# ScalarE copies the turned row maxima, first-pass slots are repacked and spread over the step, two value products stand together

## The reference

```python
scores = jnp.einsum('bqhd,bkd->bhqk', q, k) * scale
slopes = _alibi_slopes(nH)
alibi = slopes[:, None, None] * (pos_k - pos_q).astype(jnp.float32)
scores = jnp.where(causal[None, None], scores + alibi[None], NEG_INF)
probs = jax.nn.softmax(scores, axis=-1)
attn = jnp.einsum('bhqk,bkd->bqhd', probs, v).reshape(B, S, H)
return attn @ Wo
...
x = x + _L0_attn_ref(_layernorm(x, axis=-1), L0_attn_Wqkv, L0_attn_Wo)
x = x + _L0_ffn_ref(_layernorm(x, axis=-1), L0_ffn_W_base, L0_ffn_b_base, L0_ffn_W_gate, L0_ffn_A, L0_ffn_B)
```

## Time and profile before

| What | Before |
|---|---|
| Median of 3 runs | 703.57 us (703.44 to 704.35) |
| Profiled execution | 700.96 us |
| Its span in the trace | 699.2 us |
| TensorE busy | 669.7 us (96%) |
| VectorE busy | 557.4 us (80%) |
| ScalarE busy | 358.6 us (51%) |
| GpSimd busy | 216.9 us (31%) |
| Granted TensorE clock | 1.0 of full speed |

### The profile page before, as it was taken

One profiled execution on the slowest core, in us unless ns is written; L12 is line 12 of the kernel. 1 busy time (PEld: TensorE's weight loads), 2 busy tenths in 40 slices (PEclk: granted clock), 3 DMA queues, 4 the chain that ended last, 5 costly groups with the idle time before them and its releaser, 6 DMA issues.

```text
span 699.2 us, 13261 instructions
## 1 busy us (share of the span) xinstructions
PE 669.7 (96%) x4304; PEld 305.5 (44%) x4304; DVE 557.4 (80%) x1801; ACT 358.6 (51%) x511; POOL 216.9 (31%) x366
## 2 busy tenths in 40 slices
PE   3889999999999999999999999999999999999997
PEld 2434344544344444444443343433433455555553
DVE  5899889887989889898988989899881365666565
ACT  2324647567556676666666666767667411111111
POOL 0035424233332515243352231422432412222220
PEclk9999999999999999999999999999999999999999
DMA  8578108080411443080144744225200189700001
GB/s 253 130 145 137 64 2 136 30 147 28 166 54 51 60 89 108 11 131 34 41 63 94 102 81 77 49 49 94 48 18 33 52 130 170 162 30 30 31 30 60
DMA packets 42951, 56.32 MB, mean 81 GB/s; under 512 B 6648, under 2 KB 26232, under 8 KB 42752
## 3 DMA queue, kind: packets, MB, share of 16 engines
q1 hardware_dynamic: 40296, 51.27, 37.3%
q10 hardware_dynamic: 2592, 4.26, 1.8%
HBM read 35.72 MB, written 19.79 MB: 79 GB/s over the span
## 4 chain that ended last, share of the span: by engine, by line
PE 83%; DVE 10%; DMA 3%; ACT 2%; issue 1%; SPq 1%; POOL 0%; DVEq 0%; ACTq 0%; POOLq 0%
PE psum L780 20%; PE psum L732 18%; PE psum L762 13%; PE psum L808 8%; PE psum L830 7%; PE psum L678 7%; PE psum L759 5%; DVE psum L1145 3%; PE psum L825 2%; PE psum L840 2%; ACT work L965 2%; DMA x_sb<-in_x 1%; DVE negm L1150 1%; PE psum L817 1%; DMA arena<-q_dram 1%
## 5 line engine op out<-in xcount | busy, mean ns | idle before, releaser
L965 ACT ACTIVATE work<-psum 128x1024 f32<-128x1024 f32 (+1 forms) x320 | 289.0, 943 | 127.6 <-PE psum L762 108.5
L1145 DVE CUSTOM_DVE_ANT_0 psum<-psum,future 128x384 f32<-128x384 f32 (+3 forms) x512 | 237.7, 514 | 12.6 <-PE psum L732 10.4
L732 PE MATMUL psum<-k_op,arena 106*128 106x512 bf16 (+3 forms) x768 | 212.4, 328 | 9.6 <-DVE negm L1145 4.3
L1150 DVE TENSOR_REDUCE negm<-psum 128x1 f32<-128x512 f32 x256 | 168.6, 687 | 15.3 <-PE psum L732 10.9
L1318 POOL TENSOR_SCALAR_AFFINE_SELECT work<-work 128x512 f32<-128x512 f32 x128 | 81.2, 634 | 296.2 <-ACT work L965 296.2
L780 PE MATMUL psum<-work,v_op 128*32 128x512 f32 (+3 forms) x1536 | 163.5, 498 | 0.5 <-POOL work L1318 0.4
L762 PE MATMUL psum<-arena,k_op 109*128 109x512 bf16 (+3 forms) x640 | 157.3, 316 | 1.9 <-ACT work L965 0.8
L732 PEld LDWEIGHTS psum<-k_op,arena 106*128 106x128 bf16 x768 | 69.0, 97 | 128.5 <-DVE negm L1145 40.7
L678 PE MATMUL psum<-arena,wqkv_sb 128*128 128x256 f32 (+3 forms) x240 | 84.6, 453 | 1.1 <-ACT arena L887 1.1
L759 PE MATMUL psum<-arena,k_op 116*128 116x128 bf16 x512 | 84.3, 221 | 0.9 <-ACT work L965 0.9
L762 PEld LDWEIGHTS psum<-arena,k_op 109*128 109x128 bf16 x640 | 59.6, 98 | 44.5 <-ACT work L965 15.7
(11 more groups left out here) (86 smaller groups left out, 454.8 us busy)
## 6 DMA issues: line engine op xcount, KB each, us to landing
arena<-q_dram SPq DMA_DIRECT2D x96, 128.0 KB, 5.5
o_dram<-o_sb SPq DMA_DIRECT2D x32, 256.0 KB
q_dram<-arena SPq DMA_DIRECT2D x16, 384.0 KB, 4.4
arena<-o_dram SPq DMA_DIRECT2D x32, 128.0 KB, 4.6
arena<-rcp_dram SPq DMA_DIRECT2D x32, 128.0 KB, 4.9
out<-wqkv_sb ACTq DMA_DIRECT2D x16, 256.0 KB, 2.0
x_sb<-in_x SPq DMA_DIRECT2D x3, 1024.0 KB, 10.0
work<-in_x SPq DMA_DIRECT2D x3, 1024.0 KB, 18.8
```

The source lines that it names most:

```text
L732: last = nc.tensor.matmul(bank[:, a * width:(a + 1) * width], q_op[0:ROW_MAX, bass.ds(col, P)], k_op[0:ROW_MAX, b, k0:k0 + width], start=T ...
L965: nc.scalar.activation(probs[:, n % 4, heads * hp:heads * (hp + 1), 0:w], src, ACT.Exp).then_inc(exp_done, 1)
L1145: last = nc.vector.tensor_tensor_reduce(keys, keys, future[:, CH - width:CH], -1.0, 3e38, ALU.add, ALU.min, negm[:, late, 0, j * QT + t:j ...
L1150: nc.vector.tensor_reduce(dst, psum[:, bank, 0:len(js) * width].rearrange("p (a k) -> p a k", a=len(js)), AX_X, ALU.max, negate=True).then ...
```

## The change

- ScalarE copies the turned maxima (line 956) in place of VectorE, with semaphores of their own (`turn_full`, `turn_done`). The turns (line 758) are no longer slots: the early one stands behind slot 12, the late one of step k behind the third slot of step k+1, and that of the last unit ahead of step 16. A turn holds one of the three slot banks until ScalarE has copied.
- The minimum of line 1128 goes: the diagonal reduces of the late unit (line 1176) take the full block's maximum as their starting value, one column of `negm`, in place of the constant 3e38, and wait for the slot that wrote it.
- A step has 36 slots in place of 42. Diagonal blocks (j, 2) and (j, 0) share a bank, as do (j, 1) and (j+1, 1); (j, 3) stands alone. The matmuls and the columns reduced are the same.
- `SLOTS_BY` goes from 0.95 to 1.02.
- In the frame of `pe_order` the value products of the tiles with 256 and with 128 queries per head stand as one block.

The lines move: 732 becomes 746, 713 becomes 758, 759 and 762 become 782 and 785, 780 becomes 803, 965 becomes 1005, 1145 and 1150 become 1176 and 1183.

```diff
-SLOTS_BY = 0.95
+SLOTS_BY = 1.02
...
+    full = [[("full", late, ((j, t),)) for j in range(UH)] for t in range(QT)]
+    pairs = [("diag", late, ((j, 1), (j + 1, 1))) for j in range(0, UH, 2)]
+    uneven = [("diag", late, ((j, 2), (j, 0))) for j in range(UH)]
+    wide = [("diag", late, ((j, 3),)) for j in range(UH)]
+    if not late:
+        return uneven + pairs + wide
+    return full[0] + full[1] + pairs + full[2] + uneven + full[3] + wide
...
-TURN = [EARLY_SLOTS + TURN_AFTER, len(SLOTS) + 1]
-SLOTS.insert(TURN[0], ("turn", 0, None, None))
-SLOTS.insert(TURN[1], ("turn", 1, None, None))
...
+def turn_behind(k, put):
+
+
+    if put == EARLY_SLOTS + TURN_AFTER[0]:
+        return [("turn", 2 * k, None)]
+    if put == TURN_AFTER[1] and k:
+        return [("turn", 2 * k - 1, None)]
+    return []
...
-            work.append((UH * (CH - TILES[v][2]) + PV_FIXED, ("values", m, v)))
+            for tile in {2 * P: (), P: (v - 1, v)}.get(CH - TILES[v][2], (v,)):
+                work.append((UH * (CH - TILES[tile][2]) + PV_FIXED, ("values", m, tile)))
...
+            def turn_maxima(u):
+
+
+                bank, before = TURN_BANK[u]
+                bank_free(before)
+                pe.wait_ge(slot_free, NSL * (u // 2) + (NSL if u % 2 else EARLY_SLOTS))
+                nc.tensor.transpose(psum[0:UH * QT, bank, 0:P], negm[:, u % 2, 0, :], ident[:]).then_inc(turn_full, 1)
...
+            def copy_maxima(u):
+
+                act.wait_ge(turn_full, u + 1)
+                if u >= 2:
+
+                    act.wait_ge(m_split, u - 1)
+                nc.scalar.copy(m_t[:, u % 2], psum[0:UH * QT, TURN_BANK[u][0], 0:P]).then_inc(turn_done, 1)
...
-                            nc.vector.tensor_tensor(negm[:, 1, 0, :], negm[:, 1, 0, :], negm[:, 1, 1, :], ALU.min
-                                                    ).then_inc(max_late, 1)
...
+                    if k and r in (0, EARLY_SLOTS):
+
+                        dve.wait_ge(turn_full, 2 * k - 1 + late)
...
+                                last = nc.vector.tensor_tensor_reduce(keys, keys, future[:, CH - width:CH], -1.0,
+                                                                  negm[:, 1, 1, to:to + 1] if late else 3e38, ALU.add, ALU.min,
+                                                                  negm[:, late, 0, to:to + 1])
...
-                pool.wait_ge(slot_free, at_loop(NSL * (u // 2) + TURN[u % 2] + 1, i, 2 * NSL))
+                pool.wait_ge(turn_done, u + 1)
```

More of the change, by code:

```diff
@@ L165, in vector_time @@
 def vector_time(k, r):
-    kind, _, t, _ = SLOTS[r]
-    time = 450 if kind == "turn" else 680 if kind == "full" else (550, 750, 500, 700)[t]
+    kind, _, parts = SLOTS[r]
+    time = 680 if kind == "full" else sum((275, 375, 500, 700)[t] for _, t in parts)
     if r in KEY_SLOTS.get(k, ()):
@@ L217, in pe_order @@
         done += w
-        while k < NK and put < NSL - 1 and slot_due(k, put) * total <= done:
+        while k < NK and put < NSL and slot_due(k, put) * total <= done:
             out.append(("slot", k, put))
             put += 1
+            out += turn_behind(k, put)
         out.append(piece)
-    return out + [("slot", k, r) for r in range(put, NSL if k < NK else 0)]
+    for r in range(put, NSL if k < NK else 0):
+        out.append(("slot", k, r))
+        out += turn_behind(k, r + 1)
+    return ([("turn", NU - 1, None)] if k == NK else []) + out
 ORDER = [pe_order(k) for k in range(NK + 2)]
 def places():
-    slot_at, use_at, last = {}, {}, [None] * NSB
+    slot_at, use_at, turn_at, last = {}, {}, {}, [None] * NSB
     for u in range(N_FIRST):
@@ L241, in places @@
                 banks.append(bank)
+            elif what == "turn":
+                bank = banks.pop(0)
+                turn_at[a] = (bank, last[bank])
+                last[bank] = ("turn", a)
+                banks.append(bank)
             elif what == "side" and a >= N_FIRST:
@@ L267, in uses_behind @@
             piece = b
-        if what == "side" and b == len(use_parts(USES[a])) - 1:
-            out.setdefault(piece, []).append(a)
+        if what == "turn" or what == "side" and b == len(use_parts(USES[a])) - 1:
+            out.setdefault(piece, []).append((what, a))
     return out
@@ L653, in bank_free @@
                     pe.wait_ge(slot_free, n + 1)
+                elif what == "turn":
+                    pe.wait_ge(turn_done, n + 1)
                 else:
@@ L792, in step @@
                         max_slot(m, n)
+                    elif what == "turn":
+                        turn_maxima(m)
                     elif what == "scores":
@@ L1117, in _, with step @@
             KEY_PIECES = 7
-            def step(k, i=None, some=range(NSL)):
+            def step(k, some=range(NSL)):
                 for r in some:
-                    kind, late, t, js = SLOTS[r]
+                    kind, late, parts = SLOTS[r]
                     idx = NSL * k + r
                     bank = SLOT_AT[k, r][0]
-                    if kind == "turn":
-                        u = 2 * k + late
+                    if k and r in (0, EARLY_SLOTS):
+                        dve.wait_ge(turn_full, 2 * k - 1 + late)
+                    dve.wait_ge(slot_full, idx + 1)
+                    if kind == "diag":
@@ L1135, in step @@
[L1135 to L1146 removed]
+                            dve.wait_ge(slot_free, NSL * k + max(SLOTS.index(("full", 1, (part,))) for part in parts) + 1)
```

85 lines of the change are left out of this document (34 added, 51 removed).

## The result

The changed kernel takes 706.54 us (median of 6 runs, 705.61 to 708.18), the kernel before 703.41 in the runs beside it (6 runs, 702.69 to 704.35). The ratio is 1.0058, with a 95% interval of 1.0045 to 1.0071: slower by 3.2 to 5.0 us. The profiled execution took 705.61, its span is 703.8.

What follows compares the result with a forecast made beforehand. TensorE's own work was taken to set nearly all the time. Late steps +0.2, projection steps +0.55 and the loose steps with step 16 -0.1 made about +0.7 us: median 703.57 to 704.3, range 700.2 to 708.6.

Steps and rivals of the forecast that it cites:

- the likeliest case: Whole kernel: waits that go and waits that come cancel, 704.3 us, own range 702.2 to 705.8; chance 0.42.
- C: Rival, slower by VectorE: at 0.143 us a late reduce, slots come late, +0.5 a late step, 708.5 us; chance 0.15.
- 1.24 us of waits at four places: TensorE in late steps: 0.49 at (1,0), 0.30 at (5,0), 0.15 at slot 4, 0.30 at slot 30.
- +0.04: Late steps 10 to 15: 1.24 us of new waits, less 0.2 for joining, against 1.0 before; +0.04 each.
- The joined products: Value products on TensorE: one pair per step without a slot between, none in steps 1 and 2, saves 0.2 us each.
- +0.11: Projection steps 5 to 9: 0.91 us of new waits, less 0.2 for joining, against 0.6 before; +0.11 each.
- The column operand: VectorE's 16 late diagonal reduces a step read one more column: 0.06 us each, 1.0 a step.
- B: Rival, faster: the column operand hides in the reduce's own read, VectorE loses 0.85 us a step, 700.6 us; chance 0.28.
- The late maxima: Copy, split, store and load ahead of (4,0): slack shrinks from 2.87 us to 0.7, costed at nothing.
- D: Rival, slower: the late maxima take 0.7 us longer than put, (4,0) waits, 709.3 us; chance 0.14.
- -0.3 in 0 and 1, where VectorE's load decides and hardly changes: Loose steps 0 and 1, walked only roughly: 0.3 us shorter, VectorE's load deciding and hardly changing.
- Steps 2 to 4 and 16: Walked only roughly: -0.4, +0.5 and -0.2 us in 2 to 4, +0.3 in 16, whose last turn waits for VectorE.

Runs made afterwards that it cites:

- the version that beats both: Changed kernel, step 0's key split behind slots 0 to 6, normalising pieces behind 8 to 11, products joined in steps 5 to 9 alone: 700.52 us, 0.9967.
- the second trace of before: The kernel before the change, unaltered, traced once more: 704.50 us.

## Why the prediction came out as it did

The time lies in the range and the steady state comes out near the forecast; the likeliest case, no measurable change, did not come, and the slower side did, by none of the rivals. That the range holds is in part luck: its upper end was drawn for C, and what filled it was step 0, which no rival named.

- **Late steps:** forecast 1.24 us of waits at four places. After the change, in step 12 and the end of step 11:

```profile
418.40 0.28 PE L758 MATMUL psum<-ident,negm 128*16 128x128 f32 x1 [0.19 <-DVE negm L1176]
...
419.17 0.23 PE L782 MATMUL psum<-arena,k_op 116*128 116x128 bf16 x1
...
419.52 0.81 PE L746 MATMUL psum<-k_op,arena 106*128 106x384 bf16 x4
420.25 0.86 PE L803 MATMUL psum<-work,v_op 128*32 128x256 f32 x16
...
425.60 0.60 PE L785 MATMUL psum<-arena,k_op 109*128 109x512 bf16 x2
...
427.37 0.60 PE L785 MATMUL psum<-arena,k_op 109*128 109x512 bf16 x2 [0.19 <-ACT work L1005]
```

  The turn waits 0.35 for VectorE's last slots (the slot ahead of it would have ended at 418.05), (1,0) another 0.20 (419.17 in place of 418.97): 0.55 against 0.49. The turn's wait was not in the forecast; it falls into the time that (1,0) would have waited for ScalarE anyway. (5,0) waits 0.36 (forecast 0.30), the slots in the row at 419.52 0.19 (0.15), the last about 0.08 (0.30). The joined products last 0.86 in one row, apart 0.64 and 0.42. The step is 0.08 shorter, against +0.04.
- **The joined products:** the forecast took 0.2 off each step for them. Projection steps bear that out (0.18), late steps do not: with single products, in the version that beats both, they are 0.35 shorter. There one product stands behind each turn, and no wait is left at (1,0) and (5,0), which I had put down to the place of slots and turn. So joining brings these two waits with it, and the forecast's 0.2 for it had the wrong sign in late steps.
- **Step 15:** +0.83, against +0.04. It takes 29.00 with single products and 28.56 with the old spread besides (28.52 before), so joining costs 0.35 there and the spreading 0.44.
- **Projection steps:** +0.22, against +0.11; where the other 0.11 arises is not shown.
- **The column operand:** 41 ns on 512 columns and 23 on 128, against 60 assumed, so C fell, and so did B, since it is not free:

```profile
L1176 DVE CUSTOM_DVE_ANT_0 psum<-psum,future,negm 128x512 f32<-128x512 f32 x64 | 45.8, 757 | 6.1 <-PE psum L746 5.8
L1176 DVE CUSTOM_DVE_ANT_0 psum<-psum,future 128x512 f32<-128x512 f32 x64 | 44.0, 716 | 5.4 <-PE psum L746 5.0
...
L1176 DVE CUSTOM_DVE_ANT_0 psum<-psum,future,negm 128x128 f32<-128x128 f32 x64 | 22.7, 355 | 0.0
L1176 DVE CUSTOM_DVE_ANT_0 psum<-psum,future 128x128 f32<-128x128 f32 x64 | 21.2, 332 | 0.0
```

- **ScalarE's copy:** 238 ns, against 0.27 assumed.
- **The late maxima:** the split ends at 421.51 and the load is issued at 423.08; with the 1.67 of the earlier trace rows it lands at 424.75, 0.85 ahead of (4,0) at 425.60, against the 0.7 forecast. D did not come:

```profile
421.23 0.28 POOL L1341 CAST m_part<-m_rest 16x128 bf16<-16x128 f32 x1
```

```profile
423.08 0.25 SPq L552 DMA_DIRECT2D arena<-m_dram  x1
```

- **The step that failed** is the term "-0.3 in 0 and 1, where VectorE's load decides and hardly changes". Step 1 gained 1.7, which goes when VectorE copies the maxima again, but step 0 lost 5.1 (block to step 1, 49.0 for 43.8). I counted VectorE's load there and not the order of its other work, which hangs on slot numbers that the change gave a new meaning. Steps 2 to 4 and 16 came out at +0.4 together, against +0.2. The same tables have entries for steps 1, 2 and 4, which the new numbers moved too and which no run set back; whether step 2's 1.15 more comes from there is open.

Shown by experiment: the normalising pieces' place alone costs 2.6 us in the kernel before, and both tables, moved to 0 to 6 and 8 to 11, bring step 0 back to 43.6 and the ratio from 1.0058 to 1.0015. How the 5.1 divides in the changed kernel between key split, clock and normalising is not settled, since each edit alone moved the wait to the next and single traces of one order lie up to 2.1 apart.

## What to carry to other kernels

When a change renumbers the items of a schedule, look for every table that names items by number, also for work that the change does not speak of; here two untouched lines took 3 us of the time (706.5 to 703.2 with both entries moved to earlier slots). A stretch of the program that runs once can hold more than eleven repeated steps gain, so it is walked in the order listing as closely as the steady state. Where two engines can block one another, the place of a short operation counts as much as its length.

## What the runs showed of the hardware

- An operation on VectorE that takes 0.54 us alone took up to 1.58 beside GpSimd's query split, and the first small one of the group up to 1.35 in place of 0.15.
- TensorE's clock fell to 0.50 behind 2.8 us without work, in the midst of a busy stage, and stayed at 1.0 when matmuls of no use filled that wait. That brought 0.5 us to the start of step 1 and nothing measurable to the time, since the filling delayed the next slot by 1.0.
- The same kernel can have the fall in one execution and not in the next: behind a wait of 1.3 us in step 11 the clock fell to 0.50 for 3.4 us in the second trace of before and stayed at 1.0 in the first.
- One column operand costs VectorE's masked reduce 23 to 41 ns.
